# One short memset instead of two long ones between the scatters of a mixture-of-experts kernel

## What is computed

```python
t = _to_tokens(x)
t = t + _L0_ffn_ref(_ln_t(t), Wg, bg, W1, b1, W2, b2)

# _L0_ffn_ref
gate_logits = xf @ Wg + bg
top_w, top_i = jax.lax.top_k(gate_logits, 2)
top_w = jax.nn.softmax(top_w, axis=-1)
w_dense = jnp.sum(jax.nn.one_hot(top_i, E) * top_w[..., None], axis=1)
for e in range(E):
    h = jax.nn.gelu(xf @ W1[e] + b1[e], approximate=False)
    out = out + w_dense[:, e:e + 1] * (h @ W2[e] + b2[e])
```

## Time and profile before

| | us |
|---|---|
| median of 3 runs | 913.08 (911.72 to 914.72) |
| profiled execution | 913.78, of which its span 912.0 |
| PE busy | 621.5 (68%) |
| DVE busy | 693.4 (76%) |
| ACT busy | 583.5 (64%) |
| POOL busy | 416.9 (46%) |
| scatters of the expert stage (L700) | 142 of 989 ns each, 140.4 |
| memset of `placed` (L690) | 71 of 459 ns each, 32.6 |
| memset of `ranked` (L691) | 71 of 304 ns each, 21.6 |

### The profile page before, as it was taken

The page is one execution under the profiler, slowest core; times in us unless marked ns, Lnnn a source line. Parts: engine busy times, 40 slices in busy tenths (PEclk is TensorE's granted clock), DMA queues, the critical chain, the costliest instruction groups (busy, mean ns, idle before and its releaser), DMA issues. The chain is left out here.

```text
span 912.0 us, 21482 instructions
## 1 busy us (share of the span) xinstructions
PE 621.5 (68%) x6804; PEld 509.6 (56%) x6804; DVE 693.4 (76%) x2423; ACT 583.5 (64%) x1517; POOL 416.9 (46%) x556
## 2 busy tenths in 40 slices
PE   0006699999998889888888510048999999999100
PEld 0001388877777677776776410047888888888100
DVE  3699579999988998998898369038888888888153
ACT  0015489998998899788878451047788778778100
POOL 3000112221156423545645548717777777777400
PEclk9999689997999899889988555579999999999755
DMA  9933691000000000000000002122322322322499
GB/s 198 222 81 68 193 91 3 3 2 1 2 23 28 26 1 11 26 26 25 31 23 31 28 30 84 45 60 67 84 81 77 83 77 83 81 80 68 92 203 282
DMA packets 61683, 62.01 MB, mean 68 GB/s; under 512 B 20708, under 2 KB 51493, under 8 KB 59912
## 3 DMA queue, kind: packets, MB, share of 16 engines
q1 hardware_dynamic: 51592, 34.28, 18.4%
q0 software_dynamic: 8704, 17.98, 5.9%
q10 hardware_dynamic: 1280, 8.39, 4.2%
HBM read 36.18 MB, written 25.26 MB: 67 GB/s over the span
## 5 line engine op out<-in xcount | busy, mean ns | idle before, releaser
L773 ACT ACTIVATE L<-L,lmin 128x128 f32<-128x128 f32 x512 | 159.6, 398 | 0.2
L700 POOL DMA_INDIRECT expert_out<-yo,rows_all x142 | 140.4, 989 | 41.6 <-issue 21.9
L652 POOL DMA_INDIRECT routed<-pay,pos x128 | 135.6, 1060 | 42.7 <-issue 25.7
L978 DVE CUSTOM_DVE_ANT_0 L<-S,biasN,logit_scale 128x128 f32<-128x128 f32 x512 | 146.1, 346 | 6.3 <-issue 5.8
L631 POOL TENSOR_TENSOR og<-on,rden 128x256 f32<-128x256 f32 x64 | 39.6, 619 | 193.3 <-DVE on L990 191.1
L1225 DVE SCALAR_TENSOR_TENSOR hl<-hf,hscale,hh 128x512 f16<-128x512 f32 x142 | 106.7, 751 | 5.1
L864 ACT ACTIVATE hf<-S,b_sb,inv_hscale 128x256 f32<-128x256 f32 x214 | 105.0, 566 | 2.5 <-PE S L1425 1.5
L620 POOL TENSOR_TENSOR xs<-x,xs 64x512 fp32r<-64x512 f32 x32 | 40.6, 1270 | 126.8 <-ACT xs L749 106.4
L1223 DVE TENSOR_SCALAR hh<-hf,hscale 128x512 f16<-128x512 f32 x142 | 69.6, 490 | 36.7 <-ACT hf L864 29.7
L963 DVE TENSOR_TENSOR pl<-PT,ph 128x512 f16<-128x512 f32 x128 | 84.9, 685 | 13.2 <-ACT ph L768 12.5
L1440 PE MATMUL PT<-w_h,hh 128*128 x568 | 77.8, 218 | 21.5 <-DVE hl L1225 21.5
(11 more groups left out here) (232 smaller groups left out, 1828.1 us busy)
## 6 DMA issues: line engine op xcount, KB each, us to landing
rows_all<-routed SPq DMA_DIRECT2D x71, 132.0 KB
xt<-in_x SPq DMA_DIRECT2D x8, 512.0 KB, 25.6
shared<-in_L_conv_ln_w ACTq DMA_DIRECT2D x8, 512.0 KB, 12.3
shared<-in_L_conv_ln_b ACTq DMA_DIRECT2D x8, 512.0 KB, 10.5
shared<-expert_out SPq DMA_DIRECT2D x16, 256.0 KB, 11.8
pay<-expert_out SPq DMA_DIRECT2D x16, 256.0 KB, 11.3
out<-xt SPq DMA_DIRECT2D x16, 256.0 KB, 9.2
expert_out<-yo,rows_all POOLq DMA_INDIRECT x142
```

The lines of the kernel that those rows point to most:

```text
L652: pool.indirect_dma_start(routed, bass.IndirectOffsetOnAxis(ap=pos[:, slot, i:i + 1], axis=0), pay[:, i, :], None).then_inc(scattered[slot ...
L700: pool.indirect_dma_start(expert_out, bass.IndirectOffsetOnAxis(ap=row_place[t % IN_BUFS][:, k, W + 1:W + 2], axis=0), yo[t % YO_BUFS][:, ...
L773: last = nc.scalar.activation(L[p][:, h, i, :], L[p][:, h, i, :], ACT.Exp, scale=-1.0, bias=lmin[p][:, h * R + i:h * R + i + 1])
L978: last = nc.vector.tensor_tensor_reduce(out=L[p][:, h, i, :], in0=S[(4 * u + h) % 3][:, i * P:(i + 1) * P], in1=biasN[:, h, :], scale=logi ...
```

## The change

In `pause`, the memset of `placed` goes, and the memset of `ranked` covers 8 of its 256 columns. The semaphore, its count and the wait for it are as before, and so is everything else.

```diff
             def pause(t):
-                nc.gpsimd.memset(placed[:], 0.0)
-                nc.gpsimd.memset(ranked[:], 0.0).then_inc(paused, 1)
+                nc.gpsimd.memset(ranked[:, 0:E], 0.0).then_inc(paused, 1)
                 pool.wait_ge(paused, t + 1)
```

## The result

The changed kernel takes 938.33 us (median of 4 runs, 930.35 to 941.27), the kernel before 912.4 beside it (4 runs, 910.49 to 914.72). The ratio is 1.0279, with an interval of 1.0229 to 1.0328. The forecast was 940.7.

What follows compares the result with a forecast made beforehand. The prediction took the expert stage's pace to hang on where POOL's scatters lie against PE's results. 913.78 + 28.8 (held results) - 1.2 (last tiles) = 941.4, less 0.7 for the median: 940.7 us, range 908 to 985.

Steps and rivals of the forecast that it cites:

- The lateness: Expert stage: PE results due while POOL scatters reach ACT late; `fx_h` starts 1.19 us after the transposes, ACT waits 0.69.
- the first rival: Expert stage: results still go out on time, period stays 3.41, only the last tiles gain 1.2 us; 911.9, chance 0.20.
- first step: POOL between tiles: with the shorter memset the first scatter starts 0.46 us earlier, or 0.60 if `hh` doesn't hold it.
- second step: First scatter now starts 0.25 us ahead of the hidden layer's second half (L1425), so `hf` is late; 1.25 us per event.
- third step: Expert tiles: two thirds of 34 exposed tiles are hit, 23 events at 1.25 us, +28.8 us.
- fourth step: End of the expert stage: POOL is last there, so the last tiles' earlier scatters save 1.0 to 1.4 us, taken as 1.2.
- every second tile: Expert stage, sign: `hf` rows with 1 us or more of idle ACT every second tile or so.
- The sum: Whole kernel: profiled execution's 913.78 + 28.8 - 1.2 = 941.4 us; the median is 0.7 lower, so 940.7.
- No form of instruction takes longer: Whole kernel, sign: PE, DVE and POOL idle longer while instructions keep their durations; scatters may be stretched by `hl`.
- The rule that spoke against the reading: Skill's port rule: PE never waits on anyone, so moving scatters in the expert stage costs nothing; only the last tiles count.

Runs made afterwards that it cites:

- m5_by_turns: Kernel before, with SP sending tiles 0 to 14 to consecutive rows, then long memsets and the small one by turns; 918.8 us, kernel before 912.68.
- m1_modes: Kernel before in five parts: two long memsets, small memset, none, small memset with wait for the hidden layer, scatters of two tiles together; 953.64 us, kernel before 912.71.
- r1_after: The changed kernel, unchanged, run again beside the kernel before on an occasion of the 885 kind; 884.94 us against 883.08, ratio 1.0013.
- e1_no_pause: Kernel before with `pause` doing nothing, so no memset and no wait between the scatters of two tiles; 880.32 us against 884.89, ratio 0.9936.

## Why the prediction was right, and where it was not

*The lateness is real, and it is POOL's.* The forecast rested on reading ACT's wait in every tile as a matmul result that reaches its reader late because of a scatter. `m5_by_turns` shows it: 3.08 us per tile without scatters and 3.37 with them, on one occasion. How a scatter delays PE's results stays unknown; that SP's records are disturbed too, and only while POOL scatters, suggests something that the three engines share, which is argued and not shown.

*But it is not always there.* The prediction took it for a property of the kernel on this chip. On five of the seven occasions met afterwards the kernel before took some 885 us, no result was late, and the change, tried on one of them, did nearly what the first rival said: its period 3.13 against 3.10 (2.4 us more over the 70), 1.5 us less behind the last `fx_h`, 884.94 against 883.08. So the forecast of a loss holds for one kind alone; it came true because the change was measured on the kind that the profile was taken from. No row of one profile could tell this. What differs between the occasions I couldn't find.

*The scatter starts earlier (first step): right.* The memset of 8 columns is stretched by `hh` as expected and does not take the 114 ns of the earlier trace rows. Shortest, median and longest in the changed kernel:

```profile
L690 POOL MEMSET ranked<- x71: 105/258/298, 619.2 to 881.7; 128x8 f32 x71
```

Its start and the scatter's are 694.48 - 693.95 = 0.53 us apart, where 701.78 - 700.79 = 0.99 lay between them before.

*Which result is held (second step): wrong.* The prediction held the second half of the hidden layer, at the start of the first scatter, from one early tile. In the steady stretch `hf` waits 11.9 us (6.9 + 3.8 + 1.2), not 20, and mostly in short pieces: only two waits there reach 1 us. The long waits are those of `fx_h`: 31.9 us over 15. The transposes were held already, by the second scatter, with 0.69 us of ACT's time. In the kernel before, the 1.12 us between the scatters of two tiles leave room for the 0.75 after which they come through. At 0.67 us there is none, and 18 of 19 wait for another scatter. The rows for this were at hand: the earlier trace rows gives the 0.75 and the length of the pause, and the prediction asked only which result the first scatter runs into anew, not whether one already held gets out before it. `m5_by_turns` shows the same at its switches, with 0.65 us. The full rule stays open: 22 tiles with shorter gaps had no long lateness, most of them beside a longer second scatter, and 11 of them none at all. The part of `m1_modes` with the wait shows that moving the scatter behind the second half of the hidden layer, the result that the prediction named, brings only 0.39 of the lost 0.77 us per tile back (3.78 against 4.17 and 3.40).

*Count and price (third step).* 23 events at 1.25 us made 28.8. In the trace 18 of the 66 periods from the fifth tile on are over 4.5 us. Put on these alone, the 24.4 us lost are 1.36 each, about what the rows have: in 16 of the 18, 1.95 to 2.11 us of idle ACT instead of 0.69. So the count was too high and the price too low. That the two came out at 24.4 together, against 28.8, is luck. The pattern is no "every second tile" either: the long periods (4.7 to 6.7 us) come mostly every third tile, with 2.6 to 4.0 between them, and the parts of `m1_modes` and `m5_by_turns` lie between 3.63 and 4.17.

*The last tiles (fourth step): right.* -1.3 us against -1.2; a small memset leads to the scatter in 0.40 us (879.07 to 879.47), where 0.39 was worked out.

```profile
879.07 0.12 POOL L690 MEMSET ranked<- 128x8 f32 x1
879.47 0.97 POOL L699 DMA_INDIRECT expert_out<-yo,rows_all  x1 [0.28 <-issue]
```

*The sum is closer than its terms.* 941.4 was worked out for the profiled execution and 941.27 measured. 4.4 us of it were lost ahead of the first `fx_h` (606.7 against 602.3), where nothing had changed. `m1_modes` and `m5_by_turns`, of the same kind, have 604.3 and 603.6, so this is how executions vary. The expert tiles lost 4.4 less than forecast; the two misses cancel. The medians say the same with less luck: 25.9 us more (938.33 - 912.4) against the 27.6 forecast.

*"No form of instruction takes longer": wrong, without harm on the 885 kind.* The scatters take 1127 ns in the mean instead of 989, 19.7 us in all. `r1_after` has them as long (1136 ns) with no loss that can be measured, so POOL had the room on that kind, as the prediction said of its time. What the longer scatters do to held results on the 912 kind no run separates.

*The rule that spoke against the reading.* The Trainium skill (SBUF — State Buffer, section Who interferes with whom) has PE and ACT never wait on anyone. On occasions of the 885 kind the traces agree, with 0.03 and 0.05 us between transposes and `fx_h` beside a scatter; on those of the 912 kind they don't, with 1.19 to 2.28. The section is about ports of SBUF, and no run shows that the lateness has to do with one.

## What to carry to other kernels

Time that an engine spends on nothing may be room that something else needs: before an idle-looking step is shortened, ask which late result gets through in its shadow, and compare the lengths (here a gap of 1.12 us, then often 0.67, beside the 0.75 that a held result needs behind a scatter's end). Compare versions on more than one occasion, and look for a row that tells the occasions apart; here the version without any pause is the better one on one kind (0.9936) and among the worst on the other (4.17 us per tile against 3.40). Where the occasion can't be chosen, put the variants as parts into one program, with a part that repeats, and read them from one trace.

## What the runs showed of the hardware that was not expected

- The same program has two kinds of occasion, 912 and 885 us, alike up to POOL's first scatter (257.0 and 257.3 us). The granted clock doesn't explain them in the expert tiles: it is 0.871 in the mean of the kernel before and 0.874 in `e1_no_pause`, and 1.00 both from 615 to 662 and from 672 to 710 us of `m5_by_turns`, where the period is 3.08 and 3.37.
- On one kind, transposes that end beside a scatter are read by ACT 1.11 to 1.60 us late in the kernel before, and between 0.03 and 3.77 us late in the changed one, and SP's register instruction takes up to 517 ns; on the other kind they are read after 0.03 to 0.12 us, and the instruction takes at most 43 ns.
- A scatter that starts a little after `hl` on DVE is longer, on both kinds: 1.31 or 1.32 us instead of 0.97 where it starts some 0.28 us after `hl` (694.48 beside 694.20, and 69 times in `r1_after`), 1.20 where it starts some 0.4 us after (23 times in the changed kernel). One that starts at most 0.1 us after `hl` takes 0.97 (68 times in `r1_after`). `hl` reads two tiles of SBUF. The Trainium skill (SBUF — State Buffer, section Who interferes with whom) says that such an instruction contends with GpSimd's reads, and infers that the writing of descriptors isn't touched by it. The trace agrees that the two interfere; as a scatter also reads its places from SBUF (`rows_all`), it doesn't tell whether the reading or the writing was held up.
- `hh` takes 1.01 us instead of 0.49 beside three long memsets (62 of 142 times it takes about 1 us), and the period rises to 3.33 us.
